# An adaLN block with eight experts on one core: where the expert stage takes its reciprocal deviations, and when it makes its row numbers

## The reference, cut to what matters

```
h = _layernorm(x) * (1 + ca) + sa
x = x + ga * _L0_attn_ref(h, ...)              # cumulative sums, no softmax
h = _layernorm(x) * (1 + cb) + sb
x = x + gb * _L0_ffn_ref(h, ...)
...
# inside _L0_ffn_ref: each row goes to one of E = 8 experts
assign = argmax(x @ centroids.T)
xn = (x - mean) * rsqrt(var + 1e-5) * ln_g[e] + ln_b[e]
y = relu(xn @ W1[e] + b1[e]) @ W2[e] + b2[e]    # 128 -> 512 -> 128
out = x + y
```

## Time and profile before

| | us |
|---|---|
| median of 3 runs | 417.82 |
| lowest, highest | 414.26, 418.81 |
| the profiled execution's own time | 415.05 |
| its span, first to last instruction | 413.3 |

### The profile page before, as it was taken

The page is one execution under the profiler, slowest core; times in us unless marked ns, Lnnn a source line. Parts: engine busy times, 40 slices in busy tenths (PEclk is TensorE's granted clock), DMA queues, the critical chain, the costliest instruction groups (busy, mean ns, idle before and its releaser), DMA issues.

```text
span 413.3 us, 7351 instructions
## 1 busy us (share of the span) xinstructions
PE 316.5 (77%) x1837; PEld 240.4 (58%) x1837; DVE 278.5 (67%) x918; ACT 259.7 (63%) x494; POOL 265.6 (64%) x416
## 2 busy tenths in 40 slices
PE   4366788989797988786642099999999999999900
PEld 3133346545454545554432079999998888788800
DVE  4919999998999997983244346656756664666620
ACT  2158879888888888886610066766676566756400
POOL 7195145459787978586876126767676767676661
PEclk9999989999999999998555589999999999999975
DMA  7332744346498734322333723435443544341100
GB/s 214 100 83 91 224 128 132 102 131 181 139 262 218 183 121 142 106 85 102 122 125 145 244 100 103 141 110 141 117 149 94 148 123 140 102 145 32 33 0 0
DMA packets 44895, 52.23 MB, mean 126 GB/s; under 512 B 4997, under 2 KB 38431, under 8 KB 44851
## 3 DMA queue, kind: packets, MB, share of 16 engines
q1 hardware_dynamic: 38054, 34.52, 30.3%
q0 software_dynamic: 6592, 16.83, 11.8%
q10 hardware_dynamic: 208, 0.41, 0.3%
HBM read 31.32 MB, written 21.33 MB: 127 GB/s over the span
## 4 chain that ended last, share of the span: by engine, by line
issue 25%; POOL 19%; DVE 5%; PE 5%; ACT 2%; DMA 2%; POOLq 1%; SPq 0%; DVEq 0%; ACTq 0%
POOL out_dram L468 10%; POOL expert_rows L410 3%; POOL ids L463 2%; POOL zz L387 2%; PE bank L607 1%; POOL brstd L456 1%; POOL bveps L453 1%; DMA rows<-expert_rows 1%; DVE S L855 1%; PE bank L514 1%; PE bank L547 1%; DMA expert_rows<-rows,slots 1%; DVE rows L1051 1%; DVE rows L1043 1%; DVE rows L1060 1%
## 5 line engine op out<-in xcount | busy, mean ns | idle before, releaser
L468 POOL DMA_INDIRECT out_dram<-rows,ids x78 | 80.9, 1037 | 47.4 <-POOL ids L463 30.4
L726 ACT ACTIVATE rows<-bank,par 128x256 f32<-128x256 f32 x156 | 61.5, 476 | 51.3 <-PE bank L607 51.3
L410 POOL DMA_INDIRECT expert_rows<-rows,slots x64 | 64.6, 1010 | 32.0 <-DVE slots L804 17.5
L622 PE MATMUL bank<-w_all,rows 128*128 x624 | 77.0, 277 | 0.0
L607 PE MATMUL bank<-rows,early 128*128 128x256 f32 x312 | 75.5, 385 | 1.5 <-ACT rows L730 1.5
L622 PEld LDWEIGHTS bank<-w_all,rows 128*128 128x128 f32 x624 | 72.8, 192 | 2.2 <-issue 2.1
L607 PEld LDWEIGHTS bank<-rows,early 128*128 128x128 f32 x312 | 57.1, 193 | 8.8 <-ACT rows L730 2.1
L1037 DVE TENSOR_SCALAR rows<-rows,bmv,brstd 128x128 f32<-128x128 f32 x78 | 24.4, 404 | 53.8 <-POOL brstd L456 46.0
L387 POOL TENSOR_SCALAR zz<-rows,negm,rstd 128x128 f32<-128x128 f32 x64 | 31.6, 505 | 19.9 <-ACT rstd L691 19.5
L379 POOL TENSOR_SCALAR xh<-x_in,negm,rstd 128x128 f32<-128x128 f32 x64 | 29.2, 467 | 10.2 <-ACT rstd L691 9.8
L730 ACT ACTIVATE rows<-bank,par 128x256 f32<-128x256 f32 x39 | 22.6, 580 | 13.9 <-PE bank L613 13.8
(11 more groups left out here) (164 smaller groups left out, 674.5 us busy)
## 6 DMA issues: line engine op xcount, KB each, us to landing
rows<-expert_rows SPq DMA_DIRECT2D x39, 385.0 KB, 3.2
x_in<-in_L_attn_x_dram SPq DMA_DIRECT2D x16, 256.0 KB, 3.2
rows<-gates_rows SPq DMA_DIRECT2D x32, 128.0 KB, 4.9
w_all<-in_L_ffn_W_dram SPq DMA_DIRECT2D x8, 512.0 KB, 4.9
expert_rows<-pad_rows SPq DMA_DIRECT2D x9, 385.0 KB, 8.4
wg<-gates_rows SPq DMA_DIRECT2D x8, 256.0 KB, 3.3
out_dram<-rows,ids POOLq DMA_INDIRECT x78, 2.7
expert_rows<-rows,slots POOLq DMA_INDIRECT x64, 3.0
```

The source lines that it names most:

```text
L410: pool.indirect_dma_start(rows_dram, bass.IndirectOffsetOnAxis(ap=slots[:, c * CN + t:c * CN + t + 1], axis=0), rows[:, c % RR, t, :], Non ...
L468: pool.indirect_dma_start(out_rows, bass.IndirectOffsetOnAxis(ap=ids[:, k, t:t + 1], axis=0), u_sb[:, k, t, :], None, bounds_check=T - 1, ...
L622: mm = pe.matmul((ps_q, ps_k)[k][:, t * D:(t + 1) * D], hid[:, k, f, t * P:(t + 1) * P], of_expert(w2_all, e, f * D, (f + 1) * D), start=( ...
L726: r = act.activation(hid[:, k, f, :], src, ACT.Relu, bias=par[:, 2 + f, j:j + 1])
```

## The change

Three things change, all in the expert stage, and nothing ahead of it.

1. POOL no longer makes `bveps` and `brstd`. ACT makes the same value as exp(-0.5 * ln(var + eps)), with one Ln (bias `epsv`) and one Exp (scale -0.5) for each tile, three tiles ahead of the tile whose relu it does next. Its loop starts at -3 instead of -1. Ahead of the loop one table set is loaded that holds both functions.
2. POOL makes `ids` of tile `j+1` ahead of the stores of tile `j-2`, so three tiles ahead; `ids` has eight buffers instead of four.
3. DVE waits for `b_rstd` tile by tile instead of pair by pair, and its `bn_aggr` waits for the Ln that read the buffer four tiles before.

```diff
+    IR = 8
...
-    bveps = sb("bveps", [P, 4, FS])
+    blnv = sb("blnv", [P, 4, FS])
...
-    ids = sb("ids", [P, UR, FS], I32)
+    ids = sb("ids", [P, IR, FS], I32)
...
 # POOL
             for j in range(-4, NJ + 2):
-                n, u = j + 3, j - 2
-                if n % 2 == 0 and in_b(n):
-
-                    m = min(n + 2, NJ)
-                    k = slice(n % 4, n % 4 + m - n)
-                    pool.wait_ge(b_aggr, FS * m)
-                    pool.tensor_scalar(bveps[:, k, :], bmv[:, k, :, 1], LN_EPS, None, ALU.add).then_inc(b_veps, 1)
-                    pool.wait_ge(b_veps, n // 2 + 1)
-                    wait(pool, b_z, FS * (n - 2))
-                    pool.tensor_tensor(brstd[:, k, :], bveps[:, k, :],
-                                       neg_half[:, 0:FS * (m - n)].rearrange("p (a s) -> p a s", s=FS),
-                                       ALU.pow).then_inc(b_rstd, 1)
+                n, u = j + 1, j - 2
+                if in_b(n):
+                    wait(pool, s_uout[n % UR], 16 * FS * ((n - IR) // UR + 1))
+                    pool.wait_ge(s_full[n % FR], 16 * (n // FR + 1))
+                    pool.tensor_tensor(ids[:, n % IR, :], full[:, n % FR, :, D:W].bitcast(I32)
+                                       .rearrange("p s w -> p (s w)"), twice_i[:, n, :], ALU.add).then_inc(b_ids, 1)
                 if in_b(u):
                     k = u % UR
-                    wait(pool, s_uout[k], 16 * FS * (u // UR))
-                    pool.wait_ge(s_full[u % FR], 16 * (u // FR + 1))
-                    pool.tensor_tensor(ids[:, k, :], full[:, u % FR, :, D:W].bitcast(I32)
-                                       .rearrange("p s w -> p (s w)"), twice_i[:, u, :], ALU.add).then_inc(b_ids, 1)
                     pool.wait_ge(b_ids, u + 1)
                     pool.wait_ge(b_u, u + 1)
...
 # ACT
-            for j in range(-1, NJ):
-                n = j + 1
+            act.preload_act_table_set("natural_log_exp_and_others")
+            for j in range(-3, NJ):
+                n, v = j + 1, j + 3
+                if in_b(v):
+                    act.wait_ge(b_aggr, FS * (v + 1))
+                    wait(act, b_rstd, v - 3)
+                    act.activation(blnv[:, v % 4, :], bmv[:, v % 4, :, 1], ACT.Ln, bias=epsv[:, :]).then_inc(b_lnv, 1)
+                    act.wait_ge(b_lnv, v + 1)
+                    wait(act, b_z, FS * (v - 3))
+                    act.activation(brstd[:, v % 4, :], blnv[:, v % 4, :], ACT.Exp, scale=-0.5).then_inc(b_rstd, 1)
...
 # DVE
-                    dve.wait_ge(b_rstd, z // 2 + 1)
+                    dve.wait_ge(b_rstd, z + 1)
...
                     wait(dve, b_z, FS * (n - 3))
+                    wait(dve, b_lnv, n - 3)
```

More of the change, by code:

```diff
@@ L237, in build_block @@
         s_full = [sem(f"full_rows_in{i}") for i in range(FR)]
-        b_bn = sem("b_bn"); b_aggr = sem("b_aggr"); b_veps = sem("b_veps"); b_rstd = sem("b_rstd")
+        b_bn = sem("b_bn"); b_aggr = sem("b_aggr"); b_lnv = sem("b_ln_var"); b_rstd = sem("b_rstd")
         b_z = sem("b_z"); b_zTp = sem("b_zT_psum"); b_zT = sem("b_zT_ready"); b_w1 = sem("b_W1_ready")
@@ L467, in _ @@
                     for t in range(FS):
-                        pool.indirect_dma_start(out_rows, bass.IndirectOffsetOnAxis(ap=ids[:, k, t:t + 1], axis=0),
+                        pool.indirect_dma_start(out_rows, bass.IndirectOffsetOnAxis(ap=ids[:, u % IR, t:t + 1], axis=0),
                                                 u_sb[:, k, t, :], None, bounds_check=T - 1,
```

## The result

| | before | changed |
|---|---|---|
| median of 4 runs, us | 418.31 | 404.65 |
| lowest, highest | 414.26, 418.98 | 403.62, 406.35 |
| profiled execution | 415.05 | 403.62 |
| its span | 413.3 | 401.9 |

What follows compares the result with a forecast made beforehand. POOL, in series at 4.09 us a tile, was the bound, PE next at 3.734. Last store 12.2 us earlier, start 0: 402.8 from the profiled run, 405.6 from the median; 404.5 taken, range 401 to 410.

Steps and rivals of the forecast that it cites:

- The sum: Whole kernel: 12.2 us off the profiled 415.05 gives 402.8, off the median of the runs 405.6.
- POOL is the bound, PE next at 3.734: Expert stage: POOL in series takes 4.09 us a tile; with that relieved, PE keeps 3.734 to tile 36.
- The middle: PE's second layers, tile 0 to 36: that of tile 36 starts at 378.80 instead of 385.41, 6.61 us earlier.
- The end: Last tiles' stores on POOL: the last one ends at 391.9 to 392.3 instead of 404.35.
- ACT: ACT's expert loop with Ln and Exp added: shortest tile 3.44 us, 0.29 under PE's pace, weight copy at +1.45.
- the slower rival: ACT's Ln, Exp, register load and weight copy ahead of relu become the bound, slower from 4.07 us a tile; chance 0.05.
- The start: First zT on ACT, behind tile 2's Ln and Exp and a weight copy: 0 to +1.4 us, taken as 0.
- The 0.80 us: POOL's gap between ids and the first store: at most it stays 0.80, at least it falls to 0.30.
- What I gave both parts: POOL: bveps and brstd leaving saves 0.69 us a tile, to 3.41; early ids brings it to 2.9 to 3.41.
- Rival 1: ACT's handoffs cost more and its tile of 3.8 to 4.0 us bounds, still faster: 408.8 at 3.9; chance 0.09.
- rival 3: POOL stays the bound, every store paying 0.80: 3.96 us a tile, 0 to 5 us gained, about 412; chance 0.05.
- rival 4: ACT reloads the table set between Ln and Exp: 100 us more, 515; chance 0.01.

Runs made afterwards that it cites:

- experiment 6: The changed kernel itself, run again unaltered beside two others: 405.43 us, ratio to the kernel before 0.9696.
- Experiment 3: The changed kernel with brstd set to 1.0 once, without Ln, Exp and their waits: 400.40 us, ratio to before 0.9622.
- Experiment 5: The changed kernel with a second dependent Ln and Exp on ACT for each tile, result unread: 417.95 us, ratio to before 1.0005.
- experiment 7: The changed kernel with ACT copying the first-layer weights of tiles 0 and 1 ahead of its loop: 401.96 us, ratio to before 0.963.
- experiment 2: The kernel before with only the row numbers made three tiles ahead, eight buffers, pow still on POOL: 403.30 us, ratio to before 0.9663.
- experiment 4: The changed kernel without the line loading the common table set, so a load precedes every Ln and Exp: 472.98 us, ratio to before 1.1342.

## Why the prediction was right

The sum said 12.2 us off the profiled time; the profile after is 11.4 lower, 415.05 to 403.62, and 12.4 by the table, which leaves out the first stage. That the median of 404.65 lies 0.15 from the 404.5 is in part luck: the prediction only said that it would fall between 402.8 and 405.6, and the same kernel had 405.43 in experiment 6.

- **POOL is the bound, PE next at 3.734.** Right to the last digit: 134.43 us for 36 tiles. The step that carried it was to read PE's pace in the half of the stage where POOL's debt was still hidden, and not its busy share.
- **The middle**: 6.61 us forecast, 6.61 measured. Experiment 3 shows that it is PE's pace and not one that ACT happens to share: without Ln and Exp, tiles 1 to 36 are 3.73 us apart as well.
- **The end**: the last store 13.1 to 13.5 behind tile 36 forecast, 13.07 measured. The last tile's store follows with 0.30, the lower of the two values that I kept open.
- **ACT**: 3.44 us a tile forecast, 3.52 measured; copy at +1.45, measured +1.44. The relu still waits for PE, 0.22 us. Experiment 5 shows that the slower rival's turning point was right and that its distance was small.
- **The start**: 0 forecast, with up to +1.4 kept; 0.08 between the two profiles, one of each kernel, and 2.34 by experiment 6's (18.72), whose second first-layer also ran at the lower clock, so the term is the least certain of the sum: it has nothing in it for PE's clock. Counted from SP's first load, the first zT came 0.31 us earlier than before (9.25 to 8.94), against the 0 I took; it did stand behind the weight copy, and experiment 7 moved it another 1.03. What ate the 0.31 was PE's clock: the first first-layer took 3.78 us at the lower level, and 3.44 before.
- **The 0.80 us.** I kept 0.30 to 0.80 for it. In experiment 2 it is 0.17 where DVE's tile was ready early. That made no difference to the sum, since both lie under PE's pace, but it made experiment 2 surer than I had it.
- **What I gave both parts.** The prediction counted 0.69 and up to 0.5 us a tile for the two parts on POOL; by its sum the first alone gives 3.41, under PE's pace. Right, and more: the second alone is enough as well. What the second part adds to the first is the last stores, 1.05 us.

Rival 1 (ACT the bound, still faster) fell with the relu that waits for PE, rival 3 (POOL stays) with the chain; rival 4 (a reload) was not in the order, and experiment 4 puts its price at 68 us instead of the 100 that I gave.

## What to carry to other kernels

Where an engine looks 98% busy, look for a stretch where the real bound is still hidden by buffers: its pace there is what a fix can give, and the fix is worth only the distance to it, however much it takes off the old bound. An index that an indirect store needs should be made tiles ahead, since what it costs is the latency behind the wait and not its own 0.2 us. Work moved into another engine's idle time must be counted with the register loads behind it: here 0.51 us of Ln and Exp took up 0.97 us of idle time, and a second pair would have undone the gain.

## What the runs showed of the hardware

- An indirect store starts 0.85 to 0.88 us after the end of the DVE step that its last wait is for, 0.79 to 0.81 after POOL's own row numbers when those are last, 0.30 or 0.31 behind another store, and 0.17 behind a POOL instruction when its waits were satisfied earlier.
- In experiment 4 a table load on ACT is 1.28 us, 78 times over, with 0.01 to 0.02 us behind it; the 0.44 us of register load that stand in the open in the changed kernel don't show there.
- The handoff from Ln to Exp is 0.03 us (302.81 to 302.84 in the changed kernel).
- Executions of one program differ by 1.8 us by whether PE's clock has risen at its second first-layer (1.99 or 3.78 us). The first stage, the same code in all twelve traces, differs by up to 4.6, and by 3.0 between the two traces of experiment 7's kernel. What sets either I did not look into.
